# Joining the two adjacency passes of the middle layer of a three-layer graph network, with column chunks of 512, 512 and 336

## The reference

```
h = maximum(layernorm(x), 0)
h = relu(adj @ (h @ W1) + b1)        # layer 1: 512 -> 1024
h = relu(adj @ (h @ W2) + b2)        # layer 2: 1024 -> 1024
out = x + adj @ (h @ W3) + b3        # layer 3: 1024 -> 512
```

## Time and profile before

| | us |
|---|---|
| median of 3 runs | 1771.65 (1770.06 to 1772.67) |
| the profiled execution | 1772.66 |
| its span, first to last instruction | 1770.8 |

### The profile page before, as it was taken

One profiled execution on the slowest core, in us unless ns is written; L12 is line 12 of the kernel. 1 busy time (PEld: TensorE's weight loads), 2 busy tenths in 40 slices (PEclk: granted clock), 3 DMA queues, 4 the chain that ended last, 5 costly groups with the idle time before them and its releaser, 6 DMA issues. The chain is left out here.

```text
span 1770.8 us, 22422 instructions
## 1 busy us (share of the span) xinstructions
PE 1655.2 (93%) x7668; PEld 1444.3 (82%) x7668; DVE 1000.6 (57%) x1581; ACT 749.1 (42%) x1428; POOL 533.7 (30%) x651
## 2 busy tenths in 40 slices
PE   6889999999998999988999987999999999999997
PEld 6778999978787878766888876788998888989896
DVE  5554332245476566666657667565544546766664
ACT  3332221145354444555544444535334544444442
POOL 6786545213144454000005153061000422110202
PEclk9999999999999999999999999999999999999998
DMA  5557676443278889777778888787545335787774
GB/s 189 179 194 263 214 226 199 134 132 97 82 223 276 288 266 299 231 220 228 222 235 281 260 276 253 233 261 248 152 139 164 91 88 155 204 252 212 246 211 149
DMA packets 229686, 366.18 MB, mean 207 GB/s; under 512 B 26000, under 2 KB 207464, under 8 KB 229572
## 3 DMA queue, kind: packets, MB, share of 16 engines
q1 hardware_dynamic: 192222, 279.04, 52.5%
q0 software_dynamic: 13440, 46.66, 7.9%
q10 hardware_dynamic: 23910, 39.05, 6.1%
HBM read 277.30 MB, written 87.19 MB: 206 GB/s over the span
## 5 line engine op out<-in xcount | busy, mean ns | idle before, releaser
L1113 DVE TENSOR_TENSOR ring<-raw,ring 128x452 fp32r<-128x452 f32 (+1 forms) x816 | 567.5, 714 | 374.8 <-ACT ring L926 370.2
L926 ACT CAST ring<-raw 128x452 fp32r<-128x452 f32 (+1 forms) x816 | 457.6, 572 | 528.8 <-PE ps L1427 242.2
L1425 PE MATMUL ps<-ring,S 128*128 128x452 f32 x1596 | 603.7, 378 | 64.9 <-DVE ring L1113 60.5
L1426 PE MATMUL ps<-ring,S 128*128 128x452 f32 x1596 | 592.2, 371 | 0.0
L1427 PE MATMUL ps<-ring,S 128*128 128x452 f32 x1596 | 591.9, 371 | 0.0
L1425 PEld LDWEIGHTS ps<-ring,S 128*128 128x128 f32 x1596 | 302.6, 190 | 133.5 <-DVE ring L1113 86.3
L1427 PEld LDWEIGHTS ps<-ring,S 128*128 128x128 f32 x1596 | 302.6, 190 | 30.5
L1426 PEld LDWEIGHTS ps<-ring,S 128*128 128x128 f32 x1596 | 303.0, 190 | 28.4
L1425 PE MATMUL ps<-slots,still 128*128 128x452 f32 x504 | 190.2, 377 | 30.5 <-DVE still L1076 26.6
L1426 PE MATMUL ps<-slots,still 128*128 128x452 f32 x504 | 187.4, 372 | 0.0
L1427 PE MATMUL ps<-slots,still 128*128 128x452 f32 x504 | 186.7, 370 | 0.0
(11 more groups left out here) (122 smaller groups left out, 1723.6 us busy)
## 6 DMA issues: line engine op xcount, KB each, us to landing
raw<-TS SPq DMA_DIRECT2D x360, 226.0 KB, 3.2
raw<-adjT SPq DMA_DIRECT2D x306, 226.0 KB, 3.6
raw<-adjT SPq DMA_DIRECT2D x63, 452.0 KB, 4.4
TS<-made SPq DMA_DIRECT2D x30, 904.0 KB, 5.9
P<-parts ACTq DMA_DIRECT2D x48, 226.0 KB, 3.8
prep<-P POOLq DMA_DIRECT2D x48, 226.0 KB, 5.3
T<-prep POOLq DMA_DIRECT2D x48, 226.0 KB, 4.4
raw<-T SPq DMA_DIRECT2D x48, 226.0 KB, 3.1
```

Of the source, the lines that this page charges most:

```text
L926: act.copy(hi, src).then_inc(hi_done, 1)
L1113: dve.tensor_tensor(lo, src, hi.bitcast(F32), ALU.subtract).then_inc(lo_done, 1)
L1425: pe.matmul(out, st_hi, mv_hi, start=start, stop=False)
L1426: pe.matmul(out, st_hi, mv_lo, start=False, stop=False)
```

## The change

- Column chunks are 512, 512 and 336 wide instead of three of 452 (`WIDTH`, `START`); a half is 1360 columns instead of 1356.
- The two passes of layer 2 become one (`pass2`). All 1024 columns of h1 are taken as the 2x2 scheme's two sides, so a group has four PSUM banks and each moving tile is used for 4 x 3 = 12 matmuls. The seven parts are the outer loop, the three chunks the inner one. Running sums of all chunks stay in SBUF (`U`, `V`) until they are complete; a finished quadrant of a chunk is stored to `P2`.
- The stationary side of pass2 is held for two parts at a time (`odd`, `even`, 512 wide). X11 and X12 are cut as h1 is made; X22 and the four sums of h1 go to HBM (`HS`), and each comes back as ten tiles 512 wide, loaded while the part before it runs. The sums are made on tiles 512 wide (`combine1`, before 256 wide). `H1B`, `S2B`, their GpSimd sums (`prep_stationary`) and the reloading of `left` go.
- W2 comes in 28 tiles 512 wide instead of 56 of 256: three of its seven parts in the last part of pass2, four in chunk 0 of w2.
- x is loaded straight into the place that h0's `lo` takes afterwards (`xin`), all 21 blocks without waiting for one another, three ahead. `shifts` and `newton` move from GpSimd to VectorE.
- `RING1` is 2 instead of 3. The first pass's outputs are staged through six buffers instead of four. Rows of `TS` are laid out as [pair, partition, sum, column], so that a store writes four pieces a partition.
- w2, w3 and pass3 otherwise keep their order.

```diff
-W = 452
+WIDTH = (512, 512, 336)
+START = (0, 512, 1024)
 CHUNKS = 3
-RING1 = 3
-XS = 3
+RING1 = 2
+STAGES = 6
+PAIR_BUFS = 3
 LAG = 5
+INNER = 5
...
+    def pass2():
+        last_of = {}
+        def load_h1(part, t):
+            j = p.tile("s", False)
+            j.part, j.pair, j.place_freed = part, t, last_of[part - 2, t]
...
+        for part in range(7):
...
+            elif part < 6:
+                extra = [lambda t=t, i=part + 1: load_h1(i, t) for t in ORDER]
+            else:
+                extra = [lambda q=q, i=i: load_w2(i, q) for i in (X11, X12, S2) for q in range(4)]
+            half = {1: 0, 5: 0, 6: 1}.get(part)
+            for c in range(CHUNKS):
+                first = 4 * (at["rotation"] % 2)
+                at["rotation"] += 1
+                g = p.group("pass2", c, part, [first + m for m in range(4)])
...
+                for i, t in enumerate(ORDER):
+                    j = p.tile("moving", True)
+                    j.chunk, j.part, j.pair = c, part, t
...
+                    n = c * PAIRS + i
+                    if n % 3 == 1 if part < 6 else n > 3 and n % 2 == 0:
+                        spread_in(extra)
...
+    still = place("still", [P, FULL, 2, F], F32R, 0)
+    xin = place("xin", [P, FULL, 2, F], F32, 0)
...
+    odd = place("odd", [P, PAIRS, 2, F], F32R, 0)
+    even = place("even", [P, PAIRS, 2, F], F32R, HALF_ROWS)
+    V = place("V", [P, KF, HALF], F32, 2 * HALF_ROWS)
+    U = place("U", [P, KF, HALF], F32, 2 * HALF_ROWS + KF * HALF * 4)
...
-                if n >= XS:
-                    sp.wait_ge(lo1_done, xs1[n - XS].ready)
-                sp.dma_start(xs[:, n % XS, :], x[b * P:(b + 1) * P, :]).then_inc(x_in[n % XS], 16)
+                sp.dma_start(xin[:, b, 1, :], x[b * P:(b + 1) * P, :]).then_inc(x_in[b], 16)
...
+            for q in xs1[0:3]:
+                load_x(q)
...
                 dve.bn_aggr(moments[rows, 2 * n:2 * n + 2], stats[rows, half:half + 6]).then_inc(moments_done, 1)
+                dve.wait_ge(moments_done, n + 1)
+                dve.tensor_scalar(x_column(n, "v"), moments[rows, 2 * n + 1:2 * n + 2], EPS, None, ALU.add) \
+                    .then_inc(shift_done, 1)
...
+                dve.tensor_tensor(scale, step, r, ALU.mult).then_inc(newton_done, 1)
...
+                for n, j in enumerate(g.tiles):
...
+                    for m in range(KF):
+                        cols = slice(m * P, (m + 1) * P)
+                        if n == 0:
+                            bank_free(g, m)
+                        mm = three(ps[:, g.banks[m], 0:w], part[:, j.pair, 0, cols], part[:, j.pair, 1, cols],
+                                   ring[:, s, 0, 0:w], ring[:, s, 1, 0:w], start=n == 0, stop=end)
```

More of the change, by code:

```diff
@@ L137, in columns_chunk @@
     last = min(first + P, 2 * HALF) - 1
-    return max((c % HALF) // W for c in range(first, last + 1))
+    return max(sum(c % HALF >= a for a in START) - 1 for c in range(first, last + 1))
 class Pass1Tile:
@@ L387, in drain_product @@
-    def drain_product(g):
+                for t in here:
+                    j = p.tile("moving", True)
+                    j.chunk, j.part, j.pair = c, part, t
+                    g.tiles.append(j)
+                    p.release(j, g, half is None and t == here[-1])
+                    if half is not None and t == here[0]:
+                        tail_step(g, c, half)
+                    spread_in(late)
+                    p.emit_due()
+                if half is not None:
+                    if not here:
+                        tail_step(g, c, half)
+                    k = p.tile("left", True)
+                    k.chunk, k.half = c, half
+                    g.left = k
+                    p.release(k, g, True)
+                    at["tail_freed"] = g.done[-1]
+                    p.emit_due()
@@ new lines, in gcn_kernel, with e, spill, stage @@
+    b2_cols = place("b2_cols", [P, KH], F32, small + 896)
+    b3_cols = place("b3_cols", [P, KF], F32, small + 928)
+    def e(i, c=0):
+        return parts[:, i, 0:WIDTH[c]]
+    def spill(i, c):
+        return (spill_0, spill_1)[i][:, 0:WIDTH[c]]
+    def stage(s):
+        return (stage_a, stage_b)[s // 3][:, s % 3, :]
+    def columns(half, c):
+        return slice(half * HALF + START[c], half * HALF + START[c] + WIDTH[c])
+    def within(c):
+        return slice(START[c], START[c] + WIDTH[c])
@@ L1490, in block_group, with left_over @@
                     mm.then_inc(group_done if n == len(g.tiles) - 1 else slot_used, 1)
-            def product_group(g):
-                first = g.chunk == 0 and g.phase in ("pass2a", "pass3")
-                phase = "h1" if g.phase == "pass2a" else "w3"
-                side = 0 if g.part in (0, 1, 6) else 1
+            def left_over(g, ms, hi, lo, tail, side, started):
+                j = g.left
+                w = WIDTH[g.chunk]
+                pe.wait_ge(lo_done, j.cut + 1)
+                pe.wait_ge(tail_lo, g.tail[0])
+                s = j.slot % RING
+                for m in range(ms):
+                    cols = slice((side * ms + m) * P, (side * ms + m + 1) * P)
+                    if not g.tiles:
+                        bank_free(g, m)
+                    three(ps[:, g.banks[m], 0:w], hi[:, cols], lo[:, cols], ring[:, s, 0, 0:w], ring[:, s, 1, 0:w],
+                          start=not started)
+                    pe.matmul(ps[:, g.banks[m], 0:w], tail[0:REP, cols], slot_tail[0:REP, 0:w],
+                              start=False, stop=True).then_inc(group_done, 1)
@@ L1501, in product_group, with pass3_group @@
+            def pass3_group(g):
+                w = WIDTH[g.chunk]
+                for n, j in enumerate(g.tiles):
+                    if g.chunk == 0:
+                        pe.wait_ge(stat_lo, plan.stat_of["w3", j.pair, j.part])
+                    pe.wait_ge(lo_done, j.cut + 1)
+                    s = j.slot % RING
+                    end = g.left is None and n == PAIRS - 1
                     for m in range(2):
```

1350 lines of the change are left out of this document (702 added, 648 removed).

## The result

The changed kernel takes 1640.32 us (median of 4 runs, 1638.61 to 1642.07) where the kernel before took 1770.86 (4 runs, 1764.16 to 1772.67): a ratio of 0.9269, 95% interval 0.9243 to 0.9296. The profiled execution took 1642.07 us, 3.1 more than its span.

The account below looks back on a forecast made before the run. TensorE's matmuls nearly fill the span; pass2's load, cut, cut pipe loses most, 97 us. Streaming 1584.7 + 12.0 + 4 + 10 + 4.7 + 1.5 + 4 + 5 + 15 + 10.5 = 1651.4 us span, 1652 us; 8-in-10 range 1628 to 1718.

Parts of the forecast that it names:

- Streaming 1584.7: Whole kernel: all matmuls at unbroken rate take 1584.7 us, 19.0 less than before, with 157 ns a matmul at 336 columns.
- Rival 1: 336-wide matmuls: the weight load sets a floor; 190 ns gives 1725 us in all, 206.8 ns gives 1762; chance 0.12.
- rival 4: 336-wide matmuls: weight load in series, 250 ns each, 1857 us in all; slower than before from 211 ns; chance 0.03.
- First matmul 12.0: Start: x loads and ScalarE's order make the first matmul 1.5 us later, at 12.0 us (0 to +3).
- First pass 14: First pass: 4 us lost in chunk 0 and 5 us at each of two chunk boundaries, 10 together.
- rival 3: First pass: led by VectorE's small operations, each waiting for the one before; 1 us a block, 21 blocks, 1672 us; chance 0.13.
- h1 and the passage 4.7, pass2 1.5 + 4: 3.3 us before h1 and h1's 1.4 us stay; 1.5 lost in the passage from h1, 4 in pass2.
- rival 2: Pass2: the pipe stays a bound through longer loads or VectorE operations; half the loss stays, + 45, 1697 us; chance 0.12.
- w2 5: w2: 5 us lost (0 to 15), with a late tile from GpSimd's preparation and VectorE's work on W2's late parts.
- E + 30: w2, part 2 of chunk 0: TensorE asks 30 us after pass2's end (E) for a tile 2 to 4 us late.
- pass3 15: pass3: 8 us of before plus 7 in the 336-wide chunk 2, running at the pipe's limit: 15 lost (8 to 30).
- Tail 10.5: After the last matmul: a microsecond shorter with narrower last tiles, 10.5 us.

Follow-up runs that it names:

- experiment 3: A separate kernel with only TensorE matmuls, 96 at each of 18 widths from 256 to 512 columns, run once: 153.3 ns a matmul at 336, 226.9 at 512.
- experiment 8: Changed kernel with only x block 0 loaded ahead of the first adj tile and ScalarE's first roots and centring before its first adj cut: 1635.68 us.
- experiment 6: Three variants of the changed kernel: x held back again, 1672.34 us; small operations back on GpSimd, 1636.87 us; both, 1655.43 us.
- Experiment 7: Changed kernel with a finished first-pass chunk drained behind block 0 of the next chunk instead of block 1: 1631.97 us.
- Experiment 4: Changed kernel with about half of the joined pass's products left out, some 6 matmuls a moving tile, same loads, cuts and drains: 1453.87 us.
- experiment 5: Kernel before the change without the 70 reloaded tiles of the second half pass's stationary side, which multiplies with the first one's: 1738.72 us.
- experiment 1: Changed kernel with three chunks of 452 columns instead of 512, 512 and 336: 1667.81 us.
- experiments 1 and 2: Changed kernel with chunks of 452, 452 and 452 columns, 1667.81 us, and with chunks of 464, 448 and 448 columns, 1666.3 us.

## Why the prediction was right, point by point

The forecast was a span of 1651.4 us; it was 1639.0, 12.4 less. The mechanism of the largest term, pass2, was right. The sum came closer than its terms: two were 7.0 us too low together and the others 19.4 too high, and that they offset one another in part is luck. By its own terms:

- **Streaming 1584.7: measured 1576.8, -7.9.** The step was the size of one 336-wide matmul. I took 157 ns, between 153.4 (the addition of 512) and 158.5 (that of 452); the first was right. The hump of experiment 3 is why two sizes near each other gave different additions, and why the line through both pointed the wrong way. Rival 1 (a floor of 190 ns or more at 336) and rival 4 (211 or more) are excluded: 336 columns run in 153.4 ns, and 256 in 119.9. The rule of the Trainium skill weighed there, N/2.4 + 2.5 ns ("TensorE: Matmul & The Clock Gate", "Back-to-back issue gap"), gives 142.5 ns at 336 and no hump; the measurement disagrees at each of the 18 widths. The prediction left out that this section of the Trainium skill calls the rule the gap of isolated matmuls, and that it gives about 131 ns at 512 columns for a stream of weight loads and matmuls; the 226.9 ns measured here agrees with neither.
- **First matmul 12.0: 15.3, +3.3.** Above my bounds of 0 to +3, whether they are counted from 12.0 or from the 10.5 of before. I had counted SP's queue and ScalarE's order, but too low, and VectorE's queue not at all: the first adj tile landed at 7.8 us and ScalarE's first root came at 8.8, behind its cut; from 9.02 to 12.43 VectorE then did the small operations of two blocks ahead of its first adj cut (12.35) and its x cut (13.48, to 15.23). With SP's and ScalarE's order mended the first matmul comes at 12.1 (experiment 8), with the small operations on GpSimd at 12.7 (experiment 6), with both at 11.2.
- **First pass 14 (4 in chunk 0, 10 at the boundaries): 17.7, +3.7.** The 10 was near in size: from the end of chunk 0 (139.95) to the end of the pass 203.75 us against 512 x 380.1 ns = 194.6, so 9.1. Chunk 0 lost 124.7 - 512 x 0.2267 = 8.6, not 4; here is its end.

TensorE in the changed kernel (start us, us, then what it waited for, in brackets):

```profile
126.31 0.39 PE L1553 MATMUL ps<-slots,still 128*128 128x512 f32 x1
129.57 0.77 PE L1551 MATMUL ps<-slots,still 128*128 128x512 f32 x1 [2.87 <-DVE still_tail L1202]
130.13 0.63 PE L1552 MATMUL ps<-slots,still 128*128 128x512 f32 x1
130.56 0.63 PE L1553 MATMUL ps<-slots,still 128*128 128x512 f32 x1
...
136.24 0.39 PE L1551 MATMUL ps<-slots,still 128*128 128x512 f32 x1
...
139.72 0.39 PE L1576 MATMUL ps<-slot_tail,still_tail 84*128 84x512 f32 x1
141.88 0.47 PE L1551 MATMUL ps<-slots,still 128*128 128x512 f32 x1 [1.77 <-ACT stage_a L1015]
```

The rows 130.13 and 130.56 are 0.43 us apart, where full speed is 0.2267: after a gap of 3.26 us TensorE runs at the lower of its two clocks (1.2 GHz; the granted clock is 0.50 in 130 to 135.5), until about 136. The 16 distances from 129.57 to 136.24 take 6.67 us in place of 3.63, 3.0 us more, as much again as the gap. Another 2.2 us of the 8.6 is the same at the start: the first 11 distances, 15.28 to 20.00, take 4.72 in place of 2.49. What TensorE waited for is VectorE, in this row of operations, behind an adj cut that took 2.32 us, from 122.43:

```profile
124.67 1.77 DVE L1208 SCALAR_TENSOR_TENSOR still<-xin,spread,still 128x512 fp32r<-128x512 f32 x1
126.47 2.18 DVE L1216 TENSOR_TENSOR slot_tail<-raw_tail,slot_tail 20x1024 fp32r<-20x1024 f32 x1
128.68 0.74 DVE L1202 SCALAR_TENSOR_TENSOR still_tail<-rep,spread,still_tail 20x512 fp32r<-20x512 f32 x1
```

The x cut takes 1.77 us here and 0.74 where GpSimd is idle: 11 of the 21 x cuts take 1.75 to 1.78 us, each beside a subtraction of GpSimd, and the other 10 take 0.74 to 0.75. So VectorE led, as rival 3 has it, but once, at the end of chunk 0, and not a microsecond in each of 21 blocks; and not by its small operations one behind the other, which is that rival's mechanism, but by large cuts made longer beside GpSimd (x cut 1.77 and adj cut 2.32 where I had counted at most 1.04 and 1.5). ScalarE's cut ahead of that row, at 121.35, had itself waited 3.06 us for TensorE to free one of the two slots of RING1; what three slots would give in the changed kernel was not tried.
- **At the boundary** the row 141.88 is the wait I had named, for ScalarE's copy of a bank behind the cut of block 1. It is 1.77 us, and 1.47 at the second boundary, where I had a gap of 3 to 4; the rest of the 9.1 is matmuls at the lower clock behind the first (2.1 us, a wait of 0.36 among them) and smaller waits, for which I had allowed 1.5 at each. So the 10 came out by errors that offset one another. Experiment 7 puts a price on the order of that drain: 8.4 us of total time.
- **h1 and the passage 4.7, pass2 1.5 + 4: 4.8 and 2.5.** -2.9. Experiment 4 shows that with six products the pipe is a bound again, experiment 5 that 38 of the 97 us hung on the reloads. The 2.5 us that are left exclude rival 2 (half of the 97 stays). From the first h1-stationary matmul to the first of w3 it is 759.5 us, forecast 767, before 870.8.
- **w2 5: 4.6, but not by the step named.** ScalarE did wait for T (13.6 us in all, longest 2.6 at 1042, near the E + 30 = 1049 that I gave), yet TensorE did not: tiles already cut covered it. Its one longer wait in w2 is 2.34 us at 1087, for VectorE's spill between two chunks, with 1.7 us at the lower clock behind it. That the size came out is luck: the place was wrong.
- **pass3 15: 10.7.** Chunk 2 runs from 1560.1 to 1632.4, 72.3 us for 452 x 153.4 ns = 69.3: 3.0 lost where I had added 7. The tiles 336 wide landed in 2.5 us (TS) and 2.9 (adj), where I had put in the 3.2 of tiles 452 wide, so a round of the pipe was 4.1 to 4.5 us, by the same sum, against 30 x 153.4 ns = 4.6. The rest is mostly a wait of 2.92 us at 1354.6, as pass3 begins, with 1.6 us at the lower clock behind it, and two waits of 0.92 and 0.82 at 1442 and 1546.
- **Tail 10.5: 6.6.** The microsecond that I had from narrower tiles came as 0.6: from the last matmul to the end of GpSimd's last subtraction it is 2.5 us, before 3.1. The other 4.3 us were not forecast. SyncE saw the last store of outT land 1.5 us after its issue ended, before 1.9, and that is not the end: the last instruction comes 0.2 us behind the end of GpSimd's closing DRAIN. Here it is before and after, with its duration in ns and its start in us:

```profile
L575 POOLq DRAIN x1: 10524/10524/10524, 1760.1 to 1760.1; - x1
L679 POOLq DRAIN x1: 5627/5627/5627, 1633.2 to 1633.2; - x1
```

It lasts until 8.3 us behind the end of GpSimd's last subtraction before and 3.9 us after. The kernel before without its reloads (experiment 5) has 8.3 too, and the changed kernel in chunks of 452 (experiment 1) 3.9, so it is not the widths; what in the change shortened it stays open.

What I booked under the first pass as two gains, from x and from the small operations, was one. Of the forecast 119 us, the 91.5 of pass2 came as 94.5, the 19 of the widths as 27, the 16.7 of the first pass as 13.0.

## What to carry to other kernels

Where a load, cut, cut pipe is only just fast enough, count the matmuls that one moving tile feeds: doubling them emptied nearly all waits, while taking away the bunched reloads alone left 59 of 97 us. Before choosing chunk widths, measure the matmul's distance at each candidate: of the three splits tried here the even one is the dearest, by 27 us, with the one of 464, 448 and 448 level with it. Of two engines waiting in a row, ask which is late by itself: moving the small operations away from the engine that was named gained nothing, and a transfer set free and issued earlier gained 19 to 32 us.

## What the runs showed of the hardware

- **The cost of a matmul is not linear in its width.** Over N/2.4 it is 15.0 to 18.7 ns from 416 to 496 columns, against 13.3 at 336 and 13.6 at 512, with TensorE alone (experiment 3); with DMAs at work 452 and 464 columns cost the same within 1 ns (experiments 1 and 2), and 448 up to 4 ns more.
- **VectorE and GpSimd take turns.** The start of the changed kernel, both engines, start and duration in us:

```profile
11.14 1.26 POOL L1400 TENSOR_TENSOR made<-raw,made 128x512 f32<-128x512 f32 x1
11.91 0.52 DVE L1182 TENSOR_TENSOR spread<-spread 128x1 f32<-128x1 f32 x1
12.35 1.21 DVE L1224 TENSOR_TENSOR slots<-raw,slots 128x1024 fp32r<-128x1024 f32 x1
12.49 2.19 POOL L1402 TENSOR_TENSOR made<-raw,made 128x512 f32<-128x512 f32 x1
13.48 1.75 DVE L1208 SCALAR_TENSOR_TENSOR still<-xin,spread,still 128x512 fp32r<-128x512 f32 x1
```

A one-column operation of 0.16 us takes 0.52, to the end of GpSimd's subtraction at 12.40; that one's successor takes 2.19 in place of 1.26, and ends 1.12 us behind VectorE's adj cut (12.35 to 13.56); and the x cut takes 1.75 in place of 0.74, and ends 0.55 us behind GpSimd's. The same one-column operation reached 1.19 us elsewhere. Those with a single input in a tile, as L1168 (0.15 us) and L1178 (0.27), stay within 0.01 us of their shortest beside a busy GpSimd too. This agrees with the Trainium skill, "SBUF — State Buffer", section "Who interferes with whom": a VectorE instruction with two SBUF inputs and a GpSimd instruction that reads SBUF exclude one another for the whole instruction. I had costed the small operations at the 0.18 us of an operation with one input (L1048 of the earlier trace rows), which shows nothing of this.
- **A gap can cost twice.** From start to start in the changed kernel, 3.26 us at 126.3, 2.16 at 139.7, 3.22 at 343.6, 2.73 at 1084.7 and 3.31 at 1351.3 were each followed by matmuls at a granted clock of 0.50, which cost 3.0, 2.1, 1.7, 1.7 and 1.6 us more than at full clock; gaps of 1.86 us at 260.0, of 1.46 at 473.4 and of 1.3 and less in pass3 were followed by none. The length alone doesn't tell: in the kernel before, one of 2.38 us at 69.5 was followed by none, and one of 2.36 at 120.1 by 1.6 us.
